# A group of three blocks moves from VectorE to ScalarE, and the bias into VectorE's accumulator

## What is computed

```python
X0 = Xi = e                                    # (512, 39, 16)
for W, b in ((W0, b0), (W1, b1), (W2, b2)):    # b1: (128,)
    Wr = W.reshape(128, 39, fields_of_Xi)      # 39, 128, 128
    Xi = jnp.einsum('hjk,bjd,bkd->bhd', Wr, X0, Xi) + b[None, :, None]
    res.append(Xi.sum(axis=2))
h = concatenate([*res, dense_ctx], axis=1)
y = relu(relu(h @ W_top1 + b_top1) @ W_top2 + b_top2) @ W_top3
```

## Time and profile before

| | us |
|---|---|
| median of 3 runs | 722.71 (721.22 to 723.44) |
| the profiled execution | 718.87 |
| its span on the core | 717.1 |
| TensorE busy | 671.6 (94% of the span) |
| ScalarE busy | 541.1 (75%) |
| VectorE busy | 469.7 (66%) |
| GpSimd busy | 460.5 (64%) |

### The profile page before, as it was taken

The page is one execution under the profiler, slowest core; times in us unless marked ns, Lnnn a source line. Parts: engine busy times, 40 slices in busy tenths (PEclk is TensorE's granted clock), DMA queues, the critical chain, the costliest instruction groups (busy, mean ns, idle before and its releaser), DMA issues. The chain is left out here.

```text
span 717.1 us, 10090 instructions
## 1 busy us (share of the span) xinstructions
PE 671.6 (94%) x2631; PEld 481.9 (67%) x2631; DVE 469.7 (66%) x954; ACT 541.1 (75%) x1939; POOL 460.5 (64%) x445
## 2 busy tenths in 40 slices
PE   4597999999999999999999999999999999998998
PEld 4464777777677767676767677776777776774443
DVE  6245677778677777777676777786777777784000
ACT  4255797979797979888897979797979798993003
POOL 6765686877778686868686868777785736321000
PEclk9699999999999999999999999999999999998999
DMA  6664040404031312213040404040313122300000
GB/s 202 220 176 97 1 99 1 98 1 98 2 95 6 92 8 73 26 41 59 16 84 3 98 2 97 2 97 3 96 4 93 5 79 91 143 1 0 0 1 0
DMA packets 103772, 41.40 MB, mean 58 GB/s; under 512 B 86961, under 2 KB 90033, under 8 KB 103074
## 3 DMA queue, kind: packets, MB, share of 16 engines
q1 hardware_dynamic: 98594, 39.47, 21.7%
q0 software_dynamic: 5120, 1.29, 2.2%
HBM read 11.29 MB, written 2.59 MB: 19 GB/s over the span
## 5 line engine op out<-in xcount | busy, mean ns | idle before, releaser
L415 ACT ACTIVATE prod<-ps_y,xt 128x128 f32<-128x128 f32 x1792 | 498.1, 452 | 88.0 <-PE ps_y L659 79.4
L657 PE MATMUL ps_y<-w_hi,x_hi 128*128 128x512 f32 (+1 forms) x640 | 307.9, 481 | 16.2 <-DVE prod L529 14.4
L323 POOL TENSOR_TENSOR prod<-prod 128x512 f32<-128x512 f32 x128 | 165.6, 1294 | 133.6 <-ACT prod L415 132.0
L659 PE MATMUL ps_y<-w_hi,x_lo 128*128 128x512 f32 (+1 forms) x640 | 249.2, 389 | 0.0
L658 PE MATMUL ps_y<-w_lo,x_hi 128*128 128x512 f32 (+1 forms) x640 | 248.9, 389 | 0.0
L529 DVE SCALAR_TENSOR_TENSOR prod<-ps_y,xt,prod 128x128 f32<-128x128 f32 x576 | 163.8, 343 | 48.0 <-PE ps_y L659 46.2
L298 POOL DMA_INDIRECT rows<-in_table,index x160 | 153.4, 959 | 42.7 <-issue 35.7
L657 PEld LDWEIGHTS ps_y<-w_hi,x_hi 128*128 128x128 f32 x640 | 120.8, 189 | 72.3 <-DVE prod L529 26.3
L536 DVE TENSOR_REDUCE prod<-prod 128x128 f32<-128x1536 f32 x64 | 112.2, 1753 | 85.3 <-ACT prod L415 53.0
L658 PEld LDWEIGHTS ps_y<-w_lo,x_hi 128*128 128x128 f32 x640 | 120.8, 189 | 47.1 <-issue 25.5
L659 PEld LDWEIGHTS ps_y<-w_hi,x_lo 128*128 128x128 f32 x640 | 120.5, 188 | 25.3
(11 more groups left out here) (62 smaller groups left out, 235.9 us busy)
## 6 DMA issues: line engine op xcount, KB each, us to landing
room<-room SPq DMA_DIRECT2D x80, 234.0 KB
room<-room SPq DMA_DIRECT2D x48, 78.0 KB
emb_room<-rows SPq DMA_DIRECT2D x180, 5.0 KB
rows<-in_table,index POOLq DMA_INDIRECT x160
g_all<-in_L_rec_W SPq DMA_DIRECT2D x1, 2496.0 KB, 9.8
room<-room SPq DMA_DIRECT2D x16, 156.0 KB
w2t_dram<-g_all SPq DMA_DIRECT2D x1, 2496.0 KB
room<-w2t_dram SPq DMA_DIRECT2D x1, 2496.0 KB, 8.9
```

What stands on the lines that cost most here:

```text
L323: nc.gpsimd.tensor_tensor(prod[:, SLOT[a]:SLOT[a] + 2], prod[:, SLOT[a]:SLOT[a] + 2], prod[:, SLOT[b]:SLOT[b] + 2], ALU.add).then_inc(pool ...
L415: ins = nc.scalar.activation(prod[:, SLOT[k] + m // 2, :, m % 2], ps_y[:, g % YBANKS, m * H:(m + 1) * H], ACT.Copy, scale=xt[:, q % 2, ti, ...
L657: nc.tensor.matmul(y, hi, w1_hi[:, cols], start=True, stop=False)
L659: nc.tensor.matmul(y, lo, w1_hi[:, cols], start=False, stop=True).then_inc(y_made, 1)
```

## The change

Group 7, which is ScalarE's, becomes the group of three blocks, and group 8, VectorE's, gets four. ScalarE has 27 activations for a tile in place of 28, VectorE 12 blocks in place of 11. The pair that group 7 fills only by half has an empty lane, and `reduce_early` writes its result there (`EARLY_SUM = 12`, lane 1). The bias no longer lies in a pair: VectorE's first block is multiplied and added to `b1_row`. With that the pair `BIASED` is gone, `reduce_late` sums five pairs in place of six, and the copy of the bias ahead of the loop and its semaphore go.

```diff
-SIZES = [4, 4, 4, 4, 4, 4, 4, 4, 3, 4]
+SIZES = [4, 4, 4, 4, 4, 4, 4, 3, 4, 4]
...
 EARLY = slice(4, 10)
-LATE = [slice(10, 16), slice(11, 17)]
-ACCS = [10, 16]
-BIASED = 15
-PAIRS = 17
+LATE = [slice(10, 15), slice(11, 16)]
+ACCS = [10, 15]
+EARLY_SUM = 12
+PAIRS = 16
...
-                    if done < 2:
+                    if done == 1:
                         ins = nc.vector.tensor_scalar(a, y, x, None, ALU.mult)
                     else:
-                        ins = nc.vector.scalar_tensor_tensor(out=a, in0=y, scalar=x, in1=a, op0=ALU.mult, op1=ALU.add)
+                        ins = nc.vector.scalar_tensor_tensor(out=a, in0=y, scalar=x, in1=a if done else b1_row[:],
+                                                             op0=ALU.mult, op1=ALU.add)
...
-                nc.vector.tensor_reduce(prod[:, BIASED, :, 0], prod[:, EARLY].rearrange("p n h l -> p h n l"), AX_XY,
+                nc.vector.tensor_reduce(prod[:, EARLY_SUM, :, 1], prod[:, EARLY].rearrange("p n h l -> p h n l"), AX_XY,
...
-            nc.vector.tensor_copy(prod[:, BIASED, :, 1], b1_row[:]).then_inc(b1_spread, 1)
-            dve.wait_ge(b1_spread, 1)
```

More of the change, by code:

```diff
@@ L190, in build @@
         bsum_made = sem("bsum_made")
-        b1_spread = sem("b1_spread")
         ones_made = sem("ones_made")
```

## The result

The kernel after took 724.3 us (median of 22 runs, 722.25 to 726.01); the kernel before, measured beside it, 722.32 us (22 runs). The ratio is 1.0033, with a 95% interval of 1.0022 to 1.0045: slower, as forecast, but by a third of a percent (2.0 us between the medians, 2.4 by the ratio) where 3.4 us, 0.47%, were forecast.

A forecast was written before the change was run, and what follows sets the result against it. TensorE was taken as the bound, with one hole per batch behind VectorE's group 8. The terms 3.1 + 0.26 + 0.1 - 0.1 gave +3.4 us, so 726.1 us, with 722.4 to 728.2 as the range holding 0.83.

The forecast's parts named there:

- The chain by GpSimd's queue and not by ScalarE: Before group 3 of a batch's second tile: GpSimd's queue delays the early sum, then group 8, then TensorE.
- ScalarE's 0.25 us counts nothing in the 12 batches: Group 7's dropped activation gains 0 there: ScalarE's group 4 has 0.6 us to spare before GpSimd's second addition.
- a sign against its reading of GpSimd's queue: In the new profile: an early sum coming sooner behind the GpSimd addition that starts the chain would make the reading wrong.
- The fourth accumulation 0.26 us, on the path: VectorE's group 8: one more instruction delays TensorE's bank by 0.26 us, 3.1 us over the 12 batches.
- The batches without gathers: Two batches from 525 to 612 us: ScalarE ends the wait, 0.25 saved stands against 0.26 added, 2 x 0.01 = 0.
- Tile 60: In the last batch, TensorE's hole behind group 8 grows by 0.26 us; the later tiles add 0.1 in sum.
- The late sum and the bias: On VectorE: the sum over 10 blocks saves 0.27 us, the bias in the accumulation costs 0; neither moves the path.
- Rival D: TensorE's clock falls behind each hole, 12 x 3.4 = 41 us, so 767; chance 0.03.
- A: At the early sum: ScalarE ends its wait, so the shorter group 7 pays for the fourth accumulation; +0.4, 723.1 us; chance 0.17.
- B: At the hole TensorE waits for ScalarE's bank, not VectorE's, so the kernel gets faster: -3.0, 719.7 us; chance 0.05.
- C: Near the end the clock falls once more or stays low longer, 3.4 us extra, 729.5 us; chance 0.09.
- the main case: Whole kernel: the fourth accumulation lengthens the holes and ScalarE's saving gains nothing there; 726.1 us, range 725.0 to 727.9; chance 0.66.

The follow-up runs named there:

- e4: Kernel before with GpSimd's gathers spread otherwise, three instead of five in a batch's first tile, two in the third: 714.16 us, ratio 0.9894.
- e7: Kernel before with gathers spread otherwise and VectorE doing group 8 ahead of the early sum in a batch's first tile: 704.47 us, ratio 0.9749.
- e2: Kernel before with group 7's fourth activation left out, three accumulations in group 8: a batch 37.99 us, 0.06 less than before.
- e1: Kernel after with a fourth activation put back into group 7, written to a spare buffer: a batch 38.30 us; one execution 728.02 us.
- e3: Kernel before with only the sizes of groups 7 and 8 exchanged, bias and late sum as before: a batch 38.24 us; one execution 724.23 us.
- e5: Kernel after with GpSimd's gathers spread, three in a batch's first tile, two in the third: 714.78 us, ratio 0.9893; a batch 37.41 us.

## Why the prediction was right, and where it was off

**The bound and the place: right.** TensorE bounds the kernel; 12 holes before group 3 are what can move. e4 and e7 show it from the other side: with one gather fewer ahead of the addition 0.64 us of each batch went, and with the holes gone 2.5% of the time. The first batch, to which the prediction gave the same hole, has none: from group 2 to group 3 of its second tile it takes 0.91 us before and 0.89 after, so the term 0 came out of a wrong reading.

**The chain by GpSimd's queue and not by ScalarE: right, with one link overlooked.** The list of waits put 35 waits of the early sum down to ScalarE, and the rows' end times spoke for GpSimd (in the profile before the early sum starts 0.09 us behind GpSimd's addition and 1.1 or more behind ScalarE's group 6 in each of the 12 batches); e4 shows that they were right, since a change of GpSimd's queue alone took 0.63 us off the hole.

**ScalarE's 0.25 us counts nothing in the 12 batches: the term that was mis-sized.** The slack was worked out at GpSimd's second addition (0.6 us), and is there. But the chain passes the first addition too, and there, in the kernel before, GpSimd waited for ScalarE by 0.08 to 0.10 us. That wait is gone: -0.07 a batch in the profile after, -0.06 in e2, and back in e1. With it 12 x (0.26 - 0.07) + 0.3 = 2.6 us, and the loop's difference is 2.5. The prediction had a sign of it in hand: in the earlier trace rows GpSimd was 0.31 us late and the hole grew by 0.25 only, since a wait for ScalarE of 0.08 went at the same time. And it named as a sign against its reading of GpSimd's queue an early sum that comes sooner behind the start of the chain; that sign came, by 0.07 us. The reading was not wrong, but short of this link.

**The fourth accumulation 0.26 us, on the path: right.** Four take 1.12 us, three 0.86. With no gain against it, it costs 0.25 (e1).

**The batches without gathers: right.** Their holes (0.8 us for the two, in both kernels) hang on ScalarE, the two parts cancel (-0.03 and -0.02 us), and e1 and e2 show each part alone at about 0.25.

**Tile 60: right.** The hole of the earlier trace rows is 0.26 us longer, timeline of TensorE, after:

```profile
627.09 0.50 PE L656 MATMUL ps_y<-w_hi,x_hi 128*128 128x512 f32 x1 [0.52 <-DVE prod L529]
```

The rest up to the last group adds 0.02, where 0.1 was estimated.

**The late sum and the bias: right.** 1481 ns over 10 blocks (1.48 forecast), 344 and 345 ns with and without the bias (343 before), and e3 shows that neither is on the path. ScalarE is 15 us less busy (526.3; before 541.1), 16 forecast, and nothing is gained by it.

**GpSimd beside VectorE: right.** Its additions take 1297 ns on average, 1294 before.

**The clock: right for the holes.** The granted clock is 1.00 over 100 to 560 us with holes of 1.28 us of idle time, and of 1.58 in the batch of the earlier trace rows. Windows (columns as in the earlier trace rows) and timeline of TensorE, after:

```profile
100.00:560.00 460.00, 444.45 (x1804) 330.19 (x1802) 339.72 (x713) 381.33 (x1383) 349.42 (x334) 1.00 0.23 47
```

```profile
408.31 0.50 PE L656 MATMUL ps_y<-w_hi,x_hi 128*128 128x512 f32 x1 [1.58 <-DVE prod L529]
```

Rival D fell with that. What the Trainium skill ("TensorE: Matmul & The Clock Gate", Part 1: The HAM clock gate) says of an array left idle is seen here behind the gap at the end of the loop and, which the slices of the earlier trace rows hide, in the first batch, and by no hole of the loop from there on, up to 1.6 us. In the first batch TensorE waits 5.03 us for the first product (4.82 after) and goes on at 65.17 us; window of before:

```profile
64.90:68.30 3.40, 3.13 (x6) 1.83 (x6) 1.96 (x3) 0.00 (x0) 3.40 (x4) 0.50 0.23 8
```

The loop begins behind an idle time of 1.74 us in every profile, and the stretch at 0.50 of 46.6 to 50.0 us that stands near it in the profile after is missing from that of before. So one length of idle time came with a low clock and without, and that 1.5 us is safe holds for the middle of this loop, where TensorE is busy on both sides of the hole, and is not shown beyond it.

**The rivals.** A, that nothing changes because ScalarE pays, is false for this order of GpSimd's work and true in e5; its mechanism shows as the 0.07 us. The condition that the prediction set for it (the second addition within 0.06 us of group 4) was the right kind of test at the wrong one of two additions. B is false: the waits grew. C happened in the profiled execution, both ways: one more stretch at half clock in the first tile, and 10.2 us in place of 6.8 at the end. But e4, with the sizes of before, has both, so neither needs the change, and e3, with the change's sizes, has the short end.

**The number.** 12 x 0.07 = 0.8 us of the excess is the overlooked link, and 0.1 the last tiles: 3.4 becomes 2.5. The forecast of 726.1 rested on a median of 722.7, and the 22 runs of the kernel before have 722.3: 0.4 more. The last 0.5 lie between the loop's 2.5 and the 2.0 of the medians (2.4 by the ratio) and have no cause that the runs show. The mechanism was right and the size 1.4 times too large by the loop; 724.3 lies in the wide range of 722.4 to 728.2, but under the 725.0 to 727.9 that the main case was given.

## What to carry to other kernels

A wait for two engines is decided by both end times, and a chain that passes several such waits has to be checked at each of them: slack at the last does not say that there was none at the one before. Work moved from an engine ahead of the wait to one behind it costs its whole length, unless the first engine is the one that ends the wait; which it is can be changed by the order of a third engine's queue, and that order (here gathers on GpSimd and VectorE's late group) was worth some eight times the change (18.4 us between the medians of before and e7, against 2.0 to 2.5). Where the medians of the runs and two profiles disagree in size, split the profiles into preparation, loop and end before a cause is named.

## What the runs showed of the hardware

An indirect gather holds GpSimd for 0.91 to 1.02 us in the loop, and from one to the next in a row it is 1.24 to 1.32 us, in all twelve profiles; taking one out from between the two additions of a chain shortened a batch by 0.64 us, until ScalarE ended the wait.

The stretch at half clock behind the loop had two lengths, 6.8 and 10.2 us, each in six of the twelve profiles, and the choice between them went with no edit. It follows a gap of 2.13 us, of 2.06 to 2.23 over the profiles, and the length doesn't go with the gap: 2.23 us in e3 with the short stretch, 2.12 in e4 with the long one. A further stretch of 3.4 us at half clock in the loop's first tile stands in ten of the twelve, behind the same 1.74 us of idle time in each.

On one chip the kernel before took 24 us more, and in the two profiles taken there the added time lies ahead of the loop, in the wait for the first gathered rows; only ratios to the kernel before on the same chip are comparable there.
